# Loading the expert weights of a routing stage in eight paced pairs instead of two transfers

## The reference

```
x = x + 0.5 * ffn(layernorm(x));  x = x + attn(layernorm(x));  x = x + 0.5 * ffn(layernorm(x))
ffn:  top1 = argmax(x @ router_w + router_b)            # one of 8 experts per token
      a, g = split(x @ w1[e] + b1[e]);  y = (a * sigmoid(g)) @ w2[e] + b2[e],   e = top1
```

## Time and profile before

| what | value |
|---|---|
| timed runs, median of 3 | 1076.78 us |
| profiled execution, span from first to last instruction (the page gives no other time of it) | 1086.9 us |
| routing stage a, until the first sorted rows are loaded | 0 to 64.87 us |
| routing stage b, from the first scatter until the first sorted rows are loaded | 912.93 to 963.02 us |
| busy share of the span: PE, DVE, ACT, POOL | 90%, 84%, 67%, 34% |

### The profile page before, as it was taken

How to read it: one execution, slowest core, us unless ns; L and a number is a source line. 1 busy time by engine, 2 the same in 40 slices (tenths; PEclk the granted TensorE clock), 3 DMA queues, 4 the chain that set the end, 5 groups by cost and what they waited for, 6 DMA issues and landing times. The chain is left out here.

```text
span 1086.9 us, 36163 instructions
## 1 busy us (share of the span) xinstructions
PE 973.5 (90%) x11666; PEld 545.0 (50%) x11667; DVE 912.1 (84%) x1795; ACT 726.6 (67%) x1574; POOL 367.8 (34%) x481
## 2 busy tenths in 40 slices
PE   5549997778999999999999999999999997649998
PEld 4549997432333333333333333333333345649997
DVE  7558886679999999999999999999999976548886
ACT  1124443557888888888888888888888874224443
POOL 2624443212223233232232232332323244534444
PEclk9999999787999999999999999999999999569999
DMA  9722221773422122222222222222222434722221
GB/s 302 259 76 72 63 68 31 203 254 104 136 77 76 57 74 73 60 72 72 61 72 71 61 73 70 66 71 67 67 73 64 120 95 144 272 79 67 68 65 34
DMA packets 83933, 105.65 MB, mean 97 GB/s; under 512 B 15835, under 2 KB 67041, under 8 KB 83344
## 3 DMA queue, kind: packets, MB, share of 16 engines
q1 hardware_dynamic: 75888, 90.10, 27.8%
q0 software_dynamic: 5568, 12.63, 3.4%
q10 hardware_dynamic: 2432, 2.36, 0.6%
HBM read 74.14 MB, written 35.50 MB: 101 GB/s over the span
## 5 line engine op out<-in xcount | busy, mean ns | idle before, releaser
L1213 DVE TENSOR_REDUCE nmax<-psS 128x1 f32<-128x1024 f32 x507 | 595.3, 1218 | 37.1 <-PE psS L1057 28.9
L1349 ACT ACTIVATE big<-psE 128x512 f32<-128x512 f32 x1024 | 553.1, 598 | 91.1 <-PE psE L1042 88.6
L1042 PE MATMUL psE<-qop,kop 122*32 122x512 bf16 x4096 | 317.9, 384 | 4.9 <-ACT big L1349 3.4
L1423 POOL TENSOR_TENSOR big<-big,const 128x512 f32<-128x512 f32 x128 | 163.2, 1275 | 441.5 <-ACT big L1349 441.5
L1077 PE MATMUL psV<-big,vst 128*9 128x256 f32 x4096 | 265.5, 379 | 1.3
L1057 PE MATMUL psS<-maxop 32*128 32x512 bf16 x1014 | 173.6, 390 | 21.0 <-DVE nmax L1213 13.1
L1077 PEld LDWEIGHTS psV<-big,vst 128*9 128x9 f32 x4096 | 101.7, 90 | 116.3 <-issue 12.8
L1042 PEld LDWEIGHTS psE<-qop,kop 122*32 122x32 bf16 x4096 | 90.4, 95 | 130.7 <-ACT big L1349 59.4
L1057 PEld LDWEIGHTS psS<-maxop 32*128 32x128 bf16 x1014 | 47.7, 91 | 178.7 <-issue 109.0
L789 ACT ACTIVATE siga<-psGa,w1sa 128x128 f32<-128x128 f32 x156 | 44.5, 368 | 62.2 <-PE psGa L701 62.2
L789 ACT ACTIVATE sigb<-psGb,w1sb 128x128 f32<-128x128 f32 x156 | 44.5, 368 | 62.1 <-PE psGb L701 62.1
(11 more groups left out here) (194 smaller groups left out, 933.8 us busy)
## 6 DMA issues: line engine op xcount, KB each, us to landing
maxop<-qk_parts SPq DMA_DIRECT2D x256, 64.0 KB, 1.9
qop<-qk_parts SPq DMA_DIRECT2D x64, 144.0 KB
kop<-qk_parts SPq DMA_DIRECT2D x64, 144.0 KB
weighted_sums<-osum SPq DMA_DIRECT2D x64, 128.0 KB
xs<-sorted_a SPq DMA_DIRECT2D x39, 128.5 KB, 2.0
xs<-sorted_b SPq DMA_DIRECT2D x39, 128.5 KB
qk_parts<-big SPq DMA_DIRECT2D x12, 384.0 KB, 3.2
w1a<-in_w SPq DMA_DIRECT2D x1, 4128.0 KB
```

The source lines that it names most:

```text
L1042: last = nc.tensor.matmul(psE[BANK[turn]][32 * c:32 * c + 32, :], kop[b][0:TROWS, lo:lo + 32], qop[b][0:TROWS, half * HALF:(half + 1) * HALF],
L1213: nc.vector.tensor_reduce(nmax[r % 2][:, qt:qt + 1], psS[n % 2][:], AX.XY, ALU.max, negate=True).then_inc(s_max, 1)
L1349: nc.scalar.activation(prob[r % 2][:, lo:lo + HALF], psE[BANK[16 * (r % NBUF) + n]][:], ACT.Exp).then_inc(s_exp, 1)
L1423: nc.gpsimd.tensor_tensor(dst, dst, diag[:, 4 * h:4 * h + 4, :], ALU.mult).then_inc(s_diag, 1)
```

## The change

The two weight transfers are cut by expert into eight pairs, in both routing stages. Before pair e SP waits until e + 1 groups have their positions. The transfer of b2, and everything SP has behind it, comes after the eighth pair. The waits on `s_w` count 17 transfers instead of 3. The same bytes go to the same places.

```diff
+def load_weights(sp, d, g, e):
+    sp.dma_start(g.w1[:, e * W1:(e + 1) * W1], d.w1[:, e * W1:(e + 1) * W1]).then_inc(g.s_w, 16)
+    sp.dma_start(g.w2[:, e * HID:(e + 1) * HID], d.w2[:, e * HID:(e + 1) * HID]).then_inc(g.s_w, 16)
...
             fill_spare(sp, d, "a", g.s_spare["a"])
-            sp.dma_start(g.w1, d.w1).then_inc(g.s_w, 16)
-            sp.dma_start(g.w2, d.w2).then_inc(g.s_w, 16)
+            for e in range(E):
+                sp.wait_ge(s_pos, e + 1)
+                load_weights(sp, d, g, e)
             sp.dma_start(g.b2, d.b2.partition_broadcast(P)).then_inc(g.s_w, 16)
...
         @block.tensor
-            pe.wait_ge(g.s_w, 48)
+            pe.wait_ge(g.s_w, 16 * (2 * E + 1))
...
         @block.vector
-            dve.wait_ge(g.s_w, 48)
+            dve.wait_ge(g.s_w, 16 * (2 * E + 1))
...
             load_num(sp, d, g, 3)
-            sp.dma_start(g.w1, d.w1).then_inc(g.s_w, 16)
-            sp.dma_start(g.w2, d.w2).then_inc(g.s_w, 16)
+            for e in range(E):
+                sp.wait_ge(s_pos, e + 1)
+                load_weights(sp, d, g, e)
             sp.dma_start(g.b2, d.b2.partition_broadcast(P)).then_inc(g.s_w, 16)
             load_first_rows(sp, d, g, "b")
```

## The result

The changed kernel took 1085.67 us (median of 4 runs, 1084.42 to 1087.57), beside 1077.99 us of the kernel before on the same chip (4 runs): a ratio of 1.0078, 95% interval 1.0059 to 1.0097, so 7.7 us slower by the medians. The forecast was 1070.5 us, with 1078.5 us as the upper end of its range; it was wrong in sign.

What follows compares the result with a forecast made beforehand. It took POOL's scatters in the routing stages, starved by DVE stalls behind long weight packets (12.4 us lost), as the bound; 2.3 us in a plus 4.0 in b gave 6.3, so 1070.5 us, 80% range 1065 to 1078.5.

Steps and rivals of the forecast that it cites:

- the stalls cost 5.2 us: Stage a, DVE's fourth group: idle while instructions queue behind long weight packets; shorter packets cut 5.2 us to 1.6.
- term a: Routing stage a: first row load goes out earlier, POOL's path gaining 3.6 us, SP's 1.5 to 2.9; 2.3 us taken.
- term b: Routing stage b: shorter stalls let POOL's scatters be supplied sooner, gain 4.0 us, bounds 0 and 7.75.
- rival A: Both routing stages: stalls stay, belonging to the instructions there or to profiling; 0.8 to 2.1 us lost, 1078.2 us; chance 0.25.
- SP's path in a: Stage a: last pair, b2, late loads and table reads delay the first row load to 62.0 to 63.4 us; decides.
- POOL's path: Scatters supplied by DVE's positions until the first row load; in stage a gain 3.6 us, first rows at 61.3.
- covered, and costs nothing: Stage b, SP's path: last pair and b2 end about 6 us after last positions, within the scatters' 7 us.
- B: Rival, slower: load, not packet length, stalls; 4.3 to 5.8 us lost in a, about 2 in b; 1083.8 us; chance 0.12.
- C: Rival: all stalls vanish in both routing stages, gaining 4.6 us in a and 6.5 in b; 1065.7 us; chance 0.11.
- D: Rival, slower: weight pieces crawl at half of 254 GB/s, first rows 14 us late; 1091 us without b; chance 0.02.
- signs of being right: Stage a positions 4 to 6 us apart, "remote" idle under 2, POOL waits near 0.30, some 77 long packets, first rows later.
- signs of being wrong: Stalls of 4 us at the same instructions or after the fifth group, or SP's tail over 12 us after eighth positions.

## Why the prediction was wrong, step by step

**The step that failed: "the stalls cost 5.2 us", and that shorter packets take most of it away.** Of the 12.4 us of POOL's losses all but about 1.6 us are missing when the unchanged kernel runs at its usual time. So term a, 2.3 us, had nothing to win, and term b, 4.0 us, at most those 1.6, of which the changed kernel still has 1.3. The forecast noted the 10.1 us by which the profiled execution exceeds the median and that they nearly equal the losses, and gave this reading only a part of rival A's quarter of the chance. It should have been the likeliest: an execution 1% off, with stalls of 1% that no instruction of the kernel explains. What delayed that one execution stays open. With the two terms at nothing the forecast would have been no change; the 7.7 us lost are the next two steps.

**SP's path in a was seen and mis-sized.** The forecast named the mechanism: the first row load goes out a fixed time after the eighth positions, 10.6 to 12.0 us. In the unchanged kernel these come at 48.03 (47.86 + 0.17), and 12 us later is 60.0, just the time that POOL's path sets (60.05): by that sum the change would have cost nothing. Measured were 17.4 us (48.24 to 65.64). The reads took 2.1 us, inside their bounds, of which no row gave the lower one, 1.5; the landing took 15.2 instead of 9.1. From 48 to 62 us the engines moved (354 + 272 + 368) GB/s x 4 us and (139 + 49) GB/s x 1 us, 4.16 MB. Less the eight scatters still to go out, 132 KB each, this is 3.1 MB where the forecast counted 2.17. Some 0.9 MB of earlier work was still under way: the seventh pair, since pairs came 3.2 us apart at the end (45.10 and 48.27) and not 4.5, and the scatters issued just before. And beside the scatters there were 331 - 104 = 227 GB/s, not 254 (104 being 132 KB each 1.27 us). As an estimate 3.1 MB at 227 make 13.7 us, the first issue 0.6, and the rest is the uneven end, where the share falls through 0.52 and 0.19.

**That the scatters land as fast beside the loads was assumed in both stages, and was wrong.** In a the forecast let POOL's path end a fixed time after the last scatter, where its landing took 6.0 us instead of 2.7. In b it gave the scatters "some 2 to land" and called the loads "covered, and costs nothing". The pair and b2 were to be in place 6 us after the last positions; b2 landed 13.7 us after them (946.89 + 12.8 less 945.95). SP requested the rows 3.18 us after the last scatter in the unchanged kernel, 6.15 after the change. The more load bytes move beside them, the later the scatters land, which the whole transfers after eight groups show at their extreme (SP waits 13.9 us for them in b).

**Rivals.** B's 1083.8 us was nearest by number, which was luck: its mechanism was wrong, for no group was stalled, and it is the tail that grew. A was right where it put the stalls down to the profiled execution, and on SP's path as the term that is left. Its first rows at 65.6 match the 65.64 by chance, from eighth positions 6.8 us later than they came. C's eighth positions, 48.2, came true, but they come there without the change, so C had nothing to win. D's crawl did not occur with 128 partitions: the pieces kept up with the groups until the seventh pair. The fit beside D gave a pair 5.8 us; from the first issue to the second landing it took some 6.8 (0.38 + 6.4, a median of stage a). In the Trainium skill (DMA: Bandwidth & Descriptors, Anatomy of one DMA — SWDGE (gpsimd) path) that fit is for transfers that GpSimd issues; SP issues these.

**The signs set beforehand.** Most signs of being right came true: no "remote" idle, POOL's wait at 35.97 gone (that at 927.65 fell to 1.63 us), 77 packets of 8 KB and more, first rows later than the scatters allow. What they say of the stalls told nothing, since the unchanged kernel shows the same. Of the signs of being wrong one came true, SP's tail of over 12 us.

## What to carry to other kernels

Before a stall is priced, compare the profiled execution's time with the timed runs: where the excess is about the size of the stalls, profile again first. A transfer that nobody waits for yet is still best issued early, if its bytes would otherwise move in the stretch where the last results are stored and the next stage's first loads wait; what matters is that the last byte is out by then, not how evenly they flow. When something is moved behind a late event, count what else lands on the same DMA engines there, the stores that the next step waits for first.

## What the runs showed of the hardware that was not expected

- A load of 516 KB into 16 partitions took 17.1 us, the same bytes into 128 partitions 4.8 us, both issued group by group (medians of eight); with 16 partitions the engines showed a share of 0.96 to 1.03 at 145 GB/s.
- Transfers of 4128 and 2048 KB cut into pieces of 516 and 256 KB, with rows of 4.1 and 2 KB instead of 33 and 16, moved 13% less at a full share (416 to 362 GB/s, one stretch of one execution each).
- SP's wait for the scatters of stage b, the same instructions in all kernels, was 4.1 us with the loads out early, and 7.4, 11.9 and 13.9 us with the pairs, the whole transfers after five groups and after eight moving beside them.
